# When GpSimd begins to load a tile's expert weights in the second layer

## The reference

```python
x = x + attn0(layernorm(x)) * silu(ffn0(layernorm(x)))
x = x + attn1(layernorm(x)) * silu(ffn1(layernorm(x)))
```

```python
scores = sigmoid(xf @ gate_w.T)
_, topk_idx = top_k(scores + gate_bias, 2)
w = take_along_axis(scores, topk_idx); w = w / sum(w)
for e in range(8):
    we = sum(where(topk_idx == e, w, 0.0))
    h = silu(xf @ up_w[e][:176].T) * (xf @ up_w[e][176:].T)
    out = out + h @ down_w[e].T * we[:, None]
```

## Time and profile before

| | |
|---|---|
| median of 3 runs | 2081.8 us (2078.16 to 2083.91) |
| the profiled execution's own time | 2073.94 us |
| its span in the profile | 2072.2 us |
| TensorE (PE) busy | 1948.0 us, 94% of the span |
| VectorE (DVE) busy | 1403.3 us, 68% |
| ScalarE (ACT) busy | 881.7 us, 43% |
| GpSimd (POOL) busy | 682.8 us, 33% |
| DMA on GpSimd's queue (q0) | 43.94 MB, 6.4% of 16 engines |
| DMA on SyncE's queue (q1) | 173.44 MB, 27.8% of 16 engines |

### The profile page before, as it was taken

The page is one execution under the profiler, slowest core; times in us unless marked ns, Lnnn a source line. Parts: engine busy times, 40 slices in busy tenths (PEclk is TensorE's granted clock), DMA queues, the critical chain, the costliest instruction groups (busy, mean ns, idle before and its releaser), DMA issues.

```text
span 2072.2 us, 32972 instructions
## 1 busy us (share of the span) xinstructions
PE 1948.0 (94%) x11529; PEld 1429.2 (69%) x11618; DVE 1403.3 (68%) x3474; ACT 881.7 (43%) x1753; POOL 682.8 (33%) x846
## 2 busy tenths in 40 slices
PE   5989999999999999999999999999999999999998
PEld 3576676766768667676676766767677766767666
DVE  6947758577575776757766677666767577675783
ACT  3634525345252552525525254243643335343462
POOL 2634413244141441414414243132332334232341
PEclk8999999999999999999999999999999999999999
DMA  8647242262423514234232532315332163421630
GB/s 267 218 160 243 89 103 68 81 192 80 118 72 110 164 60 118 82 132 139 74 97 82 167 125 69 101 62 188 123 84 66 62 209 108 103 62 42 206 101 16
DMA packets 105261, 240.46 MB, mean 116 GB/s; under 512 B 16700, under 2 KB 26940, under 8 KB 104840
## 3 DMA queue, kind: packets, MB, share of 16 engines
q1 hardware_dynamic: 85080, 173.44, 27.8%
q0 software_dynamic: 14256, 43.94, 6.4%
q10 hardware_dynamic: 5760, 20.97, 3.0%
HBM read 179.67 MB, written 57.82 MB: 115 GB/s over the span
## 4 chain that ended last, share of the span: by engine, by line
PE 74%; DVE 13%; DMA 5%; issue 3%; ACT 1%; POOL 1%; ACTq 0%; DVEq 0%; POOLq 0%; SPq 0%
PE bank L452 22%; PE bank L616 15%; PE bank L535 10%; PE bank L501 9%; PE bank L551 7%; DVE bank L794 4%; PE bank L508 4%; DMA qring<-mneg 4%; DVE nmax L797 3%; PE bank L637 3%; PE bank L561 2%; DVE probs L812 1%; PE bank L514 1%; PE bank L463 1%; DVE xn L746 1%
## 5 line engine op out<-in xcount | busy, mean ns | idle before, releaser
L452 PE MATMUL bank<-xnT,upring 128*128 128x512 f32 (+1 forms) x2208 | 710.1, 403 | 1.3 <-DVE hbuf L837 1.3
L794 DVE CUSTOM_DVE_ANT_0 bank<-bank,mask_strip 128x512 f32<-128x512 f32 (+1 forms) x768 | 478.5, 634 | 216.6 <-PE bank L501 214.4
L696 ACT ACTIVATE probs<-bank 128x512 f32<-128x512 f32 (+1 forms) x720 | 388.3, 556 | 292.5 <-PE bank L535 266.7
L452 PEld LDWEIGHTS bank<-xnT,upring 128*128 128x128 f32 x2208 | 402.6, 192 | 59.9 <-DVE hbuf L837 9.2
L501 PE MATMUL bank<-kring,qring 127*128 127x128 f32 (+3 forms) x1280 | 378.6, 349 | 22.5 <-DVE nmax L794 13.5
L535 PE MATMUL bank<-qring,kring 128*128 128x512 f32 (+1 forms) x880 | 355.6, 408 | 38.9 <-DMA qring<-mneg 18.3
L616 PE MATMUL bank<-wdown,hbuf 128*128 128x256 f32 x1408 | 324.4, 380 | 0.0
L501 PEld LDWEIGHTS bank<-kring,qring 127*128 127x128 f32 x1280 | 225.6, 193 | 114.2 <-DVE nmax L794 64.0
L616 PEld LDWEIGHTS bank<-wdown,hbuf 128*128 128x128 f32 x1408 | 263.4, 190 | 35.5 <-issue 1.7
L535 PEld LDWEIGHTS bank<-qring,kring 128*128 128x128 f32 x880 | 167.8, 192 | 125.4 <-issue 41.9
L1663 POOL TENSOR_SCALAR_AFFINE_SELECT probs<-probs 128x512 f32<-128x512 f32 x200 | 127.8, 639 | 371.1 <-ACT probs L696 370.6
(11 more groups left out here) (165 smaller groups left out, 2184.6 us busy)
## 6 DMA issues: line engine op xcount, KB each, us to landing
upring<-up_img SPq DMA_DIRECT2D x136, 512.0 KB, 3.8
upring<-up_img ACTq DMA_DIRECT2D x40, 512.0 KB, 5.3
q_img<-probs SPq DMA_DIRECT2D x32, 512.0 KB, 3.1
kring<-k_img SPq DMA_DIRECT2D x64, 256.0 KB, 2.8
qring<-q_img SPq DMA_DIRECT2D x32, 384.0 KB, 5.0
qring<-q_img SPq DMA_DIRECT2D x192, 64.0 KB, 2.0
q_img<-probs SPq DMA_DIRECT2D x32, 256.0 KB, 3.5
k_img<-probs SPq DMA_DIRECT2D x16, 512.0 KB, 5.7
```

The source lines that it names most:

```text
L452: last = nc.tensor.matmul(out_ap, part_a(a, pa, k), part_b(b, pb, k), start=(n == 0), stop=(n == len(steps) - 1))
L696: nc.scalar.activation(pr, pr if biased else scores, ACT.Exp, scale=scale).then_inc(s_exp, 1)
L794: nc.vector.tensor_tensor_reduce(scores, scores, mask_strip[:, T - w:T], 1.0, -BIG, ALU.add, ALU.max, nmax[:, u % 2, g0, qt:qt + 1]).then_ ...
```

## The change

The load of a tile's expert weights is issued at another place of GpSimd's order. Before, `gate_load(j + 2)` stood right behind `weigh(j)`: the loads of tiles 14 and 15 in unit 4 behind the masks of kt 0 and kt 1, that of tile 16 in unit 5 behind the mask of kt 0, and so on to tile 21 in unit 10. Now each unit u from 4 to 11 begins with a wait for the first pack of exponentials of the unit and then `gate_load(TILE_AFTER[u])`: tile 14 in unit 4, tile 15 in unit 5, to tile 21 in unit 11. So the load of tile 14 comes earlier in its unit, and those of tiles 15 to 21 are put off from the middle or the end of one unit to the start of the next. In unit 4 the two `weigh` calls move too: tile 12 from behind the mask of kt 0 to the start of the unit, tile 13 from behind the mask of kt 1 to behind that of kt 0. The number of `weigh` calls and of DMAs is the same.

```diff
                     if u == U_ALL - 1 and more_batches:
                         for half in (0, 1):
                             pool_norm(pool, 0, half)
+                    pool.wait_ge(s_exp, so_far(s_exp, PACKS * u + 1))
+                    if u == UNITS[0]:
+                        weigh(pool, FRONT_TILES[-2])
+                    gate_load(pool, TILE_AFTER[u])
                     for kt in range(NT):
...
-                        if u == UNITS[0] and kt < 2:
-                            weigh(pool, FRONT_TILES[kt - 2])
-                            gate_load(pool, FRONT_TILES[kt - 2] + 2)
-                        if u > UNITS[0] and kt == 0:
-                            weigh(pool, TILE_AFTER[u - 1])
-                            gate_load(pool, TILE_AFTER[u - 1] + 2)
+                        if kt == 0:
+                            weigh(pool, FRONT_TILES[-1] if u == UNITS[0] else TILE_AFTER[u - 1])
                     if u == UNITS[0] and not b:
                         nc.gpsimd.dma_start(wdown[1][:], w1_down).then_inc(s_wd1, 16)
```

## The result

The changed kernel is faster by 0.29%: ratio to before 0.9971, 95% interval 0.996 to 0.9981, medians of 20 runs each 2071.87 and 2078.64 us. The ratio says 6.0 us (3.9 to 8.3) of 2078.6; the two medians themselves lie 6.8 us apart, inside the same interval. I had forecast 0.43%, 8.9 us.

A forecast was written before the change was run, and what follows sets the result against it. TensorE bounds the kernel, waiting for the row of maxima at the end of unit 4. Gains 6.6 + 1.1 + 0.7 + 0.5 = 8.9 us take 2081.8 to 2072.9 us; own range 2070.5 to 2075.5, 8 in 10 2068.5 to 2081.

The forecast's parts named there:

- The bottleneck and the mechanism: End of unit 4: TensorE waits 1.22 to 1.67 us in batches 0 to 6 for the row, disturbed by tile 15's load.
- Batches 1, 2, 3, 5 and 6: End of unit 4: with tile 15's load gone, the wait for the row goes almost wholly, 6.6 us gained.
- Batch 4: End of unit 4: a packet of instructions stays in the window, wait falls from 1.67 to 0.6 us, 1.1 us gained.
- Batch 7: Unit 4, GpSimd late: weighing 13 precedes kt 1's mask; TensorE may wait 0.3 us there, none for kt 2; 0.7 gained.
- Batch 0: End of unit 4: `wdown` follows the row by 0.35 us; 1.3 us gained undisturbed, 2.8 lost if caught, +0.5 taken.
- the worst case: Batch 0: row caught by `wdown` waits for all of an engine's share, sum some 6 us lower; chance 0.04.
- The forecast's own range: Whole kernel: 6.5 to 11 us gained, batch 0 from -2.8 to +1.3, batch 4 from 0.5 to 1.6; 2070.5 to 2075.5 us.
- What was costed at nothing: Units 4 to 11: tile 13's and 12's weighing and the loads of tiles 14 to 21 at new places, cost 0.
- the 2.4 us worked out: Unit 4: tile 13's weighing, moved ahead of kt 1's mask, waits 2.4 us for its load, at cost 0.
- The rival for slower: Units 5 to 10: up loads held back by expert weights reach into the row's time; 22 us lost, 9 gained; chance 0.06.
- a sign of being wrong: Profile after, units 5 to 10: up loads landing after 5 us or later would show the prediction wrong.
- the point of decision: Units 5 to 10: up loads landing some 7 us after issue, shortly ahead of the row's landing, would make rows late.

## Why the prediction came out as it did

**The bottleneck and the mechanism** held. The wait of 1.2 to 1.7 us at one boundary was the row of maxima beside tile 15's load. Moving this load alone gives the gain, putting it back takes it, and bytes from a third queue take it too.

**Batches 1, 2, 3, 5 and 6**, sized at 6.6 us: from the row's issue to the first score pack it is now 2.0 us, against 3.23, 3.34, 3.36, 3.17 and 3.66; gain 6.8 us. **Batch 4**, sized at 1.1: 3.62 to 2.92, gain 0.7; the packet of instructions stayed, as expected, with 0.97 us of wait and not 0.6. **Batch 7**, sized at 0.7: 3.19 to 2.00, gain 1.2; not even the 0.3 us for the mask of kt 1 came. The sum had tile 13's weighing as late as before, 1.09 us ahead of the row's issue (1951.73 against 1952.82), and it started 4.0 us ahead (1945.98 against 1949.98). Whether the change did that is not shown: with tile 15's load back and the weighing in its new place, it was late again (0.9 us ahead).

**Batch 0 is the term that was mis-sized**: +0.5 us forecast, 3.27 to 5.28 us measured, 2.0 us lost. The reckoning had the down weights 0.35 us behind the row; they were 0.06 us ahead. It took tile 13's load at the time that batch 2 had before and the masks at 0.65 us each. In the run the weighing could start at 182.91, 3.06 us ahead of the row's issue where I had 2.9, and the four instructions behind each other took 0.59 us a mask and 1.24 for the weighing, 3.0 us and not 3.25. A race decided by 0.4 us of such sums was worth no sign. In the four kernels in which the down weights led by 0.06, 0.09, 0.59 and 0.41 us the row took 5.2, 5.7, 6.7 and 7.6 us (the last two with 256 KB more beside or ahead of it); where they followed by 0.48 us with nothing else beside the row, it took 1.9 us, and where they followed by 0.52 us with tile 15's load beside it (two kernels) 2.8 and 3.3 us, no more than the load alone costs. The packet records show what the race is about: undisturbed, the row's packets are due 1.2 us after its issue, and in the changed kernel the first packets of the down weights, 14 KB each, began 1.24 us after it; the first ten of these took 1.0 to 1.9 us each. So the term had two values, not a middle. The lower end given, 2.8 us lost, contained it.

**The Trainium skill's rule** on how queues take turns ("DMA: Bandwidth & Descriptors", Queues, rings and completion order) was given the role of the worst case, 6 us lost. The measured row lands at 185.97 + 5.2 = 191.2 us, well before the down weights' own 185.91 + 7.8 = 193.7; the row didn't wait for all of an engine's share. The packet records show turns taken by single packets: each of the row's 16 data packets starts as a packet of the down weights ends (0.003 us before its recorded end), the next of 0.535 us starts 0.02 us later, and only behind that, 0.555 us after the data packet, comes the row's packet of 4 bytes; in batch 2 the two start 0.02 to 0.05 us apart. So the engines did switch between the queues at packets, as the rule has it; what did not come true is the worst case that I drew from it, that a row would have to wait for an engine's whole share.

**The sum**: 6.8 + 0.7 + 1.2 - 2.0 = 6.7 us at this boundary, against 8.9 forecast and 6.0 (3.9 to 8.3) measured. The profiled executions differ by less, 2072.2 - 2068.5 = 3.7 us. Of the 3.0 us between, 1.2 are other waits for rows, which came to 12.0 us in this one (16.3 - 3.34 - 0.97) against 10.8. I have not traced the rest, and can tie neither part to the change; single executions of one kernel differ by more (2067.5 to 2080.6 us after the change).

**The range and the luck.** The forecast's own range, 6.5 to 11 us gained, does not follow from the bounds named beside it: with batch 0 at -2.8 it begins at 6.6 + 1.1 + 0.7 - 2.8 = 5.6 us, and 5.0 with batch 4 at 0.5, and it ends at 6.6 + 1.6 + 0.7 + 1.3 = 10.2. The measured 6.0 us lie under the range given and inside the right one. That the time came out within 1.1 us of the forecast (2071.9 against 2072.9) is luck: the three runs that it started from had a median 3.2 us above that of twenty (2081.8 against 2078.6), and this hides a gain sized 2 to 3 us too high (8.9 against 6.0 by the ratio and 6.8 by the medians).

**What was costed at nothing** cost nothing that shows. In unit 11 of batch 2 the load is issued in the gap ahead of the mask. In unit 4 tile 13's weighing waits 0.1 to 2.1 us for its load over the eight batches (0.97 us in batch 2, against the 2.4 us worked out), and no matmul of the product waits for a mask behind it:

```profile
766.54 0.66 POOL L1613 DMA_DIRECT2D gring<-gate_img  x1
767.69 0.63 POOL L1667 TENSOR_SCALAR_AFFINE_SELECT probs<-probs 128x512 f32<-128x512 f32 x1 [0.50 <-ACT probs L696]
...
687.32 1.29 POOL L1603 TENSOR_TENSOR hbuf<-hbuf,gring 128x512 f32<-128x512 f32 x1 [0.97 <-DMA gring<-gate_img]
```

The rival for slower had a real mechanism behind it and stopped short of its point: the 115 up loads of SyncE's queue, of both layers, took 5.0 us in the median, up from 3.8. The first row below is of the kernel after, the second of the kernel before:

```profile
DMA to landing us min/median/max: 3.3/5.0/7.5
```

```profile
DMA to landing us min/median/max: 3.3/3.8/9.1
```

In units 5 to 9 alone, 40 loads, the median went from 3.7 to 5.4 us and the longest was 6.4. With only tile 15's load and the down weights moved it is 5.2 us in unit 5 and 3.7 to 4.0 in units 6 to 9, so this is the price of putting the expert weights beside them. A landing of 5 us or later stood in the prediction as a sign of being wrong, and it came: the cost of 0 held only because the up loads had more room than that, since the point of decision was 7 us. At the ends of units 5 to 10, 34 of 48 rows landed in 1.8 us, and each of the other 14 had a packet of instructions in its window.

**The better kernel** is the changed one with the down weights at the start of unit 11: 0.9946 and 0.9952 in two measurements.

## What to carry to other kernels

A small DMA that a busy engine waits for takes its time from what moves beside it: look for the one that lands in one and a half times its usual time or more, read which queues' packets are in that window, and put the large loads where no such small one is under way; here one load of eight carried the gain. When an edit makes an engine's queue earlier, follow the queue to its end, since the next large DMA on it moves up too and may take the place of the one removed. If two issues come within half a microsecond of each other by the reckoning, treat them as two cases, and fix their order or move one away.

## What the runs showed of the hardware

The row of 8 KB lands in 1.8 to 1.9 us alone: so did all 403 rows issued at the ends of units 4 to 10 in the thirteen profiles that had no packet of another queue in their window. At the end of unit 4 it lands in 3.0 to 3.5 us beside 256 KB that start up to about 1 us ahead of it, in 2.4 to 2.8 us beside such a load at the ends of units 5 to 10, and in 5.2 to 7.6 us when a load of 1792 KB is issued 0.06 to 0.6 us ahead. The same 256 KB issued 2.0 us ahead did nothing to it in five batches, though they were in flight when the row was issued: its own packets start only 1.2 us after the issue. And 1792 KB issued 0.48 us behind it didn't either.

A single packet of instructions, 16 KB in queue q8, goes with a landing of 2.5 to 3.6 us: 124 of the 125 rows that had one in their window, and nothing of GpSimd's or ScalarE's queue, took that long. In batch 4 of the changed kernel 15 of the row's 16 data packets start 1.22 to 1.36 us after the issue and the last one at 1.74, as the packet of instructions, in flight from 0.43 to 1.75, ends. That is 0.4 of the 0.92 us by which this row is late; the other 0.5 us pass between the row's last packet and its landing, and no record shows why. Such a packet stands beside this row in twelve of the thirteen profiles.
